# Causal attention: the v projection put between the first and second transposes, and the q projection behind the second

## What is computed

```python
q = (x @ Wq).reshape(B, T, H, dh).transpose(0, 2, 1, 3)
k = (x @ Wk).reshape(B, T, H, dh).transpose(0, 2, 1, 3)
v = (x @ Wv).reshape(B, T, H, dh).transpose(0, 2, 1, 3)
logits = jnp.einsum('bhqd,bhkd->bhqk', q, k)
logits = logits + causal[None, None] + _pos_bias(rel_pos_bias, T)[None]
logits = logits / dh
probs = jax.nn.softmax(logits, axis=-1)
out = jnp.einsum('bhqk,bhkd->bhqd', probs, v)
return out.transpose(0, 2, 1, 3).reshape(B, T, H * dh) @ Wo + bo
```

## Time and profile before

| | before |
|---|---|
| median of three runs | 2877.6 us |
| profiled execution | 2880.57 us |
| its span, first to last instruction | 2878.8 us |
| PE matmul busy, share of the span | 2673.1 us, 93% |
| DVE busy | 2149.5 us, 75% |
| ACT busy | 2110.9 us, 73% |
| POOL busy | 1597.9 us, 56% |
| mean granted TensorE clock | 0.980 |

### The profile page before, as it was taken

The page is one execution under the profiler, slowest core; times in us unless marked ns, Lnnn a source line. Parts: engine busy times, 40 slices in busy tenths (PEclk is TensorE's granted clock), DMA queues, the critical chain, the costliest instruction groups (busy, mean ns, idle before and its releaser), DMA issues. The chain is left out here.

```text
span 2878.8 us, 78477 instructions
## 1 busy us (share of the span) xinstructions
PE 2673.1 (93%) x24208; PEld 2000.9 (70%) x24208; DVE 2149.5 (75%) x5783; ACT 2110.9 (73%) x6207; POOL 1597.9 (56%) x1939
## 2 busy tenths in 40 slices
PE   6999999999999999999959999999787999999786
PEld 3666666666666666666638888887676888888575
DVE  4677676776767667677749999998457999999565
ACT  5777676776767767677739999999345999999642
POOL 2434343433434344344348999997226999999521
PEclk9999999999999999999989999999899999999998
DMA  2000000000000000000031111111111111111112
GB/s 68 5 9 9 10 5 8 7 9 9 5 8 7 9 9 5 8 7 5 5 106 38 36 37 37 37 36 37 42 29 34 38 36 37 37 37 36 45 32 74
DMA packets 128405, 75.57 MB, mean 26 GB/s; under 512 B 80197, under 2 KB 110737, under 8 KB 128145
## 3 DMA queue, kind: packets, MB, share of 16 engines
q1 hardware_dynamic: 125824, 70.22, 9.9%
q10 hardware_dynamic: 2320, 2.20, 0.3%
HBM read 17.58 MB, written 8.41 MB: 9 GB/s over the span
## 5 line engine op out<-in xcount | busy, mean ns | idle before, releaser
L282 POOL TENSOR_SCALAR L<-L,rinv 128x128 f32<-128x128 f32 (+3 forms) x1024 | 522.6, 532 | 765.1 <-DVE rinv L465 765.1
L348 ACT ACTIVATE L<-L,nmax 128x128 f32<-128x128 f32 (+3 forms) x1024 | 564.9, 555 | 13.5 <-DVE nmax L452 4.3
L452 DVE CUSTOM_DVE_ANT_0 L<-bank,bias_tab 128x128 f32<-128x128 f32 (+3 forms) x1024 | 473.3, 485 | 100.6 <-PE bank L568 96.7
L860 ACT ACTIVATE f_L<-bank,f_nmax,f_rn 128x128 f32<-128x128 f32 x1024 | 458.5, 477 | 8.7 <-DVE f_nmax L987 5.2
L837 POOL TENSOR_TENSOR f_rn<-f_ssq,f_mhalf 128x16 f32<-128x16 f32 x128 | 404.4, 3160 | 32.6 <-DVE f_ssq L971 28.2
L819 POOL TENSOR_TENSOR f_qkr<-f_ab 128x256 f32<-128x256 f32 x512 | 401.4, 813 | 12.2 <-DVE f_ab L938 12.2
L589 PE MATMUL bank<-ident,L 128*128 128x128 f32 x2560 | 358.6, 280 | 2.2 <-DVE PT L214 1.0
L938 DVE TENSOR_TENSOR f_ab<-bank,f_tab 128x512 f32<-128x512 f32 x512 | 347.9, 680 | 6.7 <-ACT f_sq L850 6.7
L589 PEld LDWEIGHTS bank<-ident,L 128*128 128x128 f32 x2560 | 294.2, 144 | 45.7 <-DVE PT L214 13.0
L214 DVE COPY PT<-bank 128x512 f32<-128x512 f32 x384 | 264.8, 690 | 59.5 <-PE bank L589 56.8
L607 PE MATMUL bank<-PT,v 128*64 128x512 f32 (+3 forms) x2048 | 303.9, 439 | 0.0
(11 more groups left out here) (145 smaller groups left out, 6438.2 us busy)
## 6 DMA issues: line engine op xcount, KB each, us to landing
f_vm<-f_v SPq DMA_DIRECT2D x224, 128.0 KB, 2.3
f_hs<-xf SPq DMA_DIRECT2D x132, 32.0 KB
f_hs<-xf SPq DMA_DIRECT2D x132, 31.8 KB
xb<-in_L_attn_x SPq DMA_DIRECT2D x16, 256.0 KB, 2.8
out<-yacc SPq DMA_DIRECT2D x32, 128.0 KB, 1.8
f_hs<-xf SPq DMA_DIRECT2D x32, 128.0 KB
out<-f_acc SPq DMA_DIRECT2D x4, 1024.0 KB, 7.5
f_hs<-xf SPq DMA_DIRECT2D x32, 127.0 KB
```

The costliest lines, as they stand in the source:

```text
L282: nc.gpsimd.tensor_scalar(t, t, rinv[:, h % RING, a, i:i + 1], 1.0, ALU.mult, ALU.mult).then_inc(s_N, 1)
L348: nc.scalar.activation(t, t, ACT.Exp, bias=nmax[:, p % RING, a, i:i + 1], scale=-1.0, accum_out=rsum[:, p % RING, a, i:i + 1]).then_inc(s_ ...
L452: nc.vector.tensor_tensor_reduce(out=L[:, p % RING, a, LOFF[i]:LOFF[i] + (i + 1) * P], in0=ps_s[a][i % 2][:, 0:(i + 1) * P], in1=bias_tab[ ...
L860: nc.scalar.activation(L[:, ot % 2, a, k, :], ps_s[a][:, k * P:k * P + P], ACT.Exp, bias=nmax[:, ot % 2, a, k:k + 1], scale=rn[:, ot % 2, ...
```

## The change

Each slot's v goes between transposes 1 and 2, where q was, and q goes between transposes 3 and scores 2. On ACT v's copy takes the place that q's had, after exp (0,0), and q's copy goes behind fill 3. Which piece of v a slot makes is shifted by one: slot p now makes piece p + 2, or piece p - 6 of the next batch, and two pieces, not three, are made ahead of the first slot. The wait on v's eviction goes in front of q and that on `s_XTl` in p = 5 in front of v; the transposed x of p = 4 now waits for k's low part, not for v. DVE's list is unchanged.

```diff
--- before.py
+++ after.py
@@ -91,9 +91,9 @@
 
 def value_item(b, p, par):
 
-    if p >= 5:
-        return (b + 1, p - 5, 1 - par) if has_scores(b) and has_next(b) else None
-    return (b, p + 3, par) if has_scores(b) else None
+    if p >= 6:
+        return (b + 1, p - 6, 1 - par) if has_scores(b) and has_next(b) else None
+    return (b, p + 2, par) if has_scores(b) else None
 
 
 def y_step(b, p, par):
@@ -324,7 +324,7 @@
             xT_high(0, 0)
             high((0, 0, 0), s_q, q_hi, s_qh)
             high((0, 0, 0), s_k, k_hi, s_kh)
-            for n in range(3):
+            for n in range(2):
                 value_out((0, n, 0))
             for n in range(H // 2):
                 act.wait_ge(s_tabp, n + 1)
@@ -350,11 +350,13 @@
 
                 fills(1)
                 exps(0, 0)
-                if lead is not None:
-                    high(lead, s_q, q_hi, s_qh)
+                if item is not None:
+                    value_out(item)
                 exps(0, 1)
                 exps(1, 0)
                 fills(3)
+                if lead is not None:
+                    high(lead, s_q, q_hi, s_qh)
                 exps(1, 1)
                 exps(2, 0)
                 if COPIER[4] == "A":
@@ -371,8 +373,6 @@
 
                     act.wait_ge(s_Y, at(b, HP, p - 4))
                     nc.scalar.activation(o[:, h % 4, :], ps_o[:], ACT.Copy).then_inc(s_O, 1)
-                if item is not None:
-                    value_out(item)
                 if p == 4 and has_scores(b) and has_next(b):
                     xT_high(b + 1, 1 - par)
             pair_slots(act, slot, 4)
@@ -627,16 +627,17 @@
                 scores(1)
                 transposes(0)
                 transposes(1)
-                if lead is not None:
-                    if not has_next(b) and p > 5:
-                        pe.wait_ge(s_Ya, at(b, HP, p - 4))
-                    else:
-                        pe.wait_ge(s_Ve, at(b, HP, p + 3))
-                    if p == 5:
-                        pe.wait_ge(s_XTl, at(b, 1, 2) if has_next(b) else at(b, 1, 1))
-                    project(lead, wq_hi, wq_lo, s_q)
+                if p == 5 and has_next(b):
+                    pe.wait_ge(s_XTl, at(b, 1, 2))
+                if item is not None:
+                    pe.wait_ge(s_kl, at(b, HP, p + 1))
+                    values_of(item)
                 transposes(2)
                 transposes(3)
+                if lead is not None:
+                    if item is not None:
+                        pe.wait_ge(s_Ve, at(b, HP, p + 3))
+                    project(lead, wq_hi, wq_lo, s_q)
                 scores(2)
                 scores(3)
                 if lead is not None:
@@ -650,12 +651,8 @@
                         pe.wait_ge(s_Ya, at(b, HP, p - 3))
                     project(lead, wk_hi, wk_lo, s_k)
                 heads_out()
-                if item is not None:
-                    if lead is not None:
-                        pe.wait_ge(s_kl, at(b, HP, p + 2))
-                    values_of(item)
                 if p == 4 and has_scores(b) and has_next(b):
-                    pe.wait_ge(s_Ve, at(b, HP, p + 4))
+                    pe.wait_ge(s_kl, at(b, HP, p + 2))
                     transpose_x(b + 1)
             pair_slots(pe, slot, 4)
 
```

## The result

The changed kernel takes 2907.64 us (median of 4 runs, 2903.14 to 2914.6) against 2877.6: ratio 1.0103, interval 1.0091 to 1.0115, so it is 1.0% slower. The profiled execution took 2904.99 us, span 2903.2 against 2878.8: +24.4 us, where the forecast had +22.7. The four runs go by the mean clock: 2903.1 at 0.984, 2905.0 at 0.982, 2910.3 at 0.980, 2914.6 at 0.978.

A forecast was written before the change was run, and what follows sets the result against it. The tensor engine's own order sets the time, with y held by q's late copy (chance 0.78). 26.1 - 7.0 + 2.1 + 1.5 gives +22.7 us on the median of 2877.6, forecast 2900, range 2887 to 2914.

The forecast's parts named there:

- The ordinary slot: Slots without special work: q's copy behind fill 3 starts at 4.72, y at 6.10, slot grows 0.30 to 10.97.
- rival 1: Ordinary slots: evictions hide, y at 5.66, slots of 10.55, total -24 us to 2854; chance 0.11.
- The prediction's own chain: Eviction of a projection: copy 1.00 after its start, then 0.60, 0.03, 0.69, 0.06; successor 2.38 after the projection.
- v's hand-over: From v's copy on ScalarE to q on the tensor engine: bounded by 0.06 and 0.13, taken as 0.13.
- Behind y: Rest of an ordinary slot: distances stay, k 1.67 after y, the next scores 3.20 after k.
- Rival 2: Before k: its wait for the y addition, worth 0.23, takes up the delay; total 2880, no change; chance 0.06.
- Rival 3: Tensor engine: new gaps make the clock fall in one slot in eight, +24 us, 2924; chance 0.05.
- p = 4 and p = 5: 15 slots each: p = 4 changes by -0.47 a slot (-7.0 us), p = 5 by +0.14 (2.1 us).
- ordinary slots: 87 of the 128 slots, each 0.30 longer: 26.1 us.
- The start: Before the loop one v fewer, -2.3 us; slots 0 and 1 about +0.8 each for uncovered evictions.
- p = 7 and 0: Slots around the six back edges: +7.2 us, with 0 taken for the back edges themselves, 5 us either way.
- The price of a copy: ScalarE: rows give 0.47 to 0.51 per copy; the skill's 0.52 would put q's copy about 0.1 later, total near 2910.

The follow-up runs named there:

- e1: The changed kernel with q's copy before fill 3 on ScalarE instead of behind it; ratio 1.0092.
- e2: e1 with v's copy also moved before exp (0,0) on ScalarE; ratio 1.0043.
- e12: The changed kernel with ScalarE's copies of q, k and v waiting for their projection alone, in their late places; ratio 1.0097.
- e8: e6 with ScalarE's copies of q, k and v waiting for their projection alone; ratio 0.9940, 2862.46 us.
- e6: e5 plus v's copy before exp (0,0), q's copy before exp (1,0), and the statistics' sums before q's subtraction in p = 2; ratio 1.0005.
- e4: The kernel before with the new order in slot p = 4 alone, ScalarE's copies to match; ratio 0.9986, median 2873.75 us.
- e3: The changed kernel with the next batch's statistics before q's subtraction on VectorE in p = 2, not at the slot's end; ratio 1.0115.
- e5: e1 with the projection's wait written last in ScalarE's helpers for the copies of q, k and v; ratio 1.0073.

## Why the prediction was right

**The ordinary slot** came out as worked out, 10.97, by the step it named: q's copy at 4.73 (forecast 4.72) behind fill 3, y at 6.10. e1, e2 and e12 show that it is that place; rival 1 asked for copies that start earlier, at 2.62 and 4.28. The prediction's own chain ruled it out, since the data of v and q would be there at 2.73 and 3.35 + 1.00 = 4.35; so its chance of 0.11 was too high. e8 comes nearest to it: 10.62 instead of 10.55, because y does not follow q there by less than 2.38 (q at 3.37, y at 5.75).

**v's hand-over** was taken at 0.13 from the p = 4 slot; it is 0.05, near the lower bound, and q starts at 3.53 instead of 3.62. It changed nothing, since y hangs on the queue of ScalarE. The other gap, before y, was larger for it: 0.26, not 0.17 (6.10 less 3.53, 0.89 and 1.42).

**Behind y** all kept its distance (k 1.68 behind y, scores 3.19 behind k). Rival 2, that k's wait would absorb the delay, is refuted: the wait of k for the y addition is still there (the last row of the waits above: 40.3 us in 123 slots). Rival 3 is refuted for ordinary slots: the clock was 1.00 over the 100 us above, and so it was from 61 to 300 us, up to the first back edge.

**p = 4 and p = 5** came within 0.6 us each in the sum.

**What was too small**: p = 3 (+7.1 for +4.5). The step "ordinary slots" counted p = 3 among the 87, with no look at what VectorE does at the end of p = 2; with 0.90 less between its k subtraction and the next scores, 1.6 us of statistics no longer fit. p = 6 (+6.4 for +4.5): in every other batch the slot takes 11.23. Behind v's wait an `ALU_OP` and an `EVENT_SEMAPHORE` stand ahead of its copy there in every batch, but 0.35 passes between the two in the longer slots (461.44 and 461.79) and 0.07 in the others (554.25 and 554.33); why is open, and with one wait it is gone (e12). **The start** (+3.4 for -0.1): slots 0 and 1 were priced at full clock. Here are the clocks of these stretches in the changed kernel, where the second slot starts at 45.6 and the fourth at 66.9:

```profile
38.00:46.00 8.00, 5.59 (x40) 3.63 (x39) 5.47 (x19) 5.93 (x18) 0.00 (x0) 1.00 0.00 0
46.00:58.00 12.00, 9.83 (x49) 6.53 (x47) 6.12 (x27) 7.33 (x23) 4.56 (x10) 0.67 0.01 3
58.00:62.00 4.00, 4.00 (x20) 3.19 (x20) 2.04 (x6) 2.87 (x10) 3.64 (x7) 0.70 0.00 0
```

With no transposes to fill the waits, the tensor engine was busy 5.59 of 8 us, and then the clock fell to 1.2 GHz for a part of the next stretches. The second slot takes 10.1 us, where it took 6.8, and the third 11.2 for 9.4. The same slots in other kernels tell what of it is the clock; the second slot of e6, then that of e4, whose order there is the old one:

```profile
45.15:52.96 7.81, 5.42 (x33) 3.32 (x34) 5.03 (x20) 6.27 (x20) 4.11 (x8) 1.00 0.02 4
...
47.05:55.20 8.15, 6.65 (x34) 4.14 (x34) 5.21 (x19) 6.36 (x20) 4.10 (x8) 0.79 0.02 4
```

At full clock e6 takes 7.8 and, in the third slot, 9.7: 1.1 and 0.3 more than the kernel before, about what the forecast had (0.8 and 0.3). So 3 to 4 us of the start are the clock, an estimate (10.12 + 11.17 less 7.81 + 9.72 is 3.8, a little of it e6's earlier copies), and rival 3 did happen in that place. Of the eight kernels with the new order in every slot seven had the clock fall there, e6 did not; of the five that start in the old order e4 alone did (8.15 for 6.75). So the new order makes it likely here but does not decide it alone, and what does was not tried. The Trainium skill (TensorE: Matmul & The Clock Gate, A second HAM failure mode: psum-queue depth-cycling) says that short idles between groups of matmuls which cycle through PSUM banks make the clock swing. The trace of the changed kernel agrees at its start; that of e6, busy 5.42 of 7.81 us there at a clock of 1.00, does not, nor do the gaps of 0.18 and 0.26 us in the ordinary slots, which ran at 1.00.

**What was too large**: p = 7 and 0 (+2.3 for +7.2). The slots behind the back edges were at half clock for shorter in this execution than in the one before (their sum over six is 71.2 against 76.5). This share differs with no edit near it: e3, whose edit is in p = 2, has 75.0. What the change does to it was not tried.

**The price of a copy.** The Trainium skill's figure (ScalarE: Activation LUTs, What ACT_TABLE_LOAD costs) gave an estimate of 0.52 and q's copy 0.1 later; the trace has 0.48 between fill 3 and q's copy, and 4.73. The measurement decides.

## What to carry to other kernels

When several products share one PSUM bank, look not at how busy the evicting engine is but at what stands ahead of the eviction in its queue at that moment: ScalarE was idle 30% of the time, and still q's copy came late by its place. Moving work on the bottleneck engine needs the order of the other engines' queues worked out again, slot by slot, with the odd slots (here the one with statistics) on their own. And a wait that is always met long before may still cost when it, or the value that it needs, is handled behind the wait that matters: leave it out where order on the producing engine implies it.

## What the runs showed that was not expected

- A copy started 1.00 us behind its projection's first matmul where the copy itself carries the projection's wait, 1.08 where an `EVENT_SEMAPHORE` ahead of it does (e5, e6), and 1.14 where an `ALU_OP` does and an `EVENT_SEMAPHORE` follows (e1). Which it is depends on the order in which the waits are written and on the loop's values, and is seen only among the sequencer's instructions. e6 (1.0005) and e8 (0.9940) differ in nothing but the waits. Their medians are 18.5 us apart, where 7 were expected, their profiled executions 12.3; of these 8.2 stand in the slots p = 1 to 6 (sums of 981.6 and 973.4), and of the rest, in p = 7 and 0, a part is the clock behind the back edges.
- The hand-over from ScalarE's copy to the tensor engine took 0.05 in the ordinary slot and 0.13 before the x transposes. Why the two differ was not tried.
